# Block products of W_in and W_out in token halves of 256 columns

## What is computed

```python
# layer 0, scale and shift from a small MLP of a noise encoding of t
out = silu(scale * layer_norm(x, gamma, beta) + shift)     # mean and variance over tokens and features
out = out @ W_in + b_in                                     # 512 x 512
out = silu(scale * layer_norm(out, gamma, beta) + shift)
x2 = out @ W_out + b_out + x                                # 512 x 512
# layer 1, one expert per batch, picked by an index
h = gelu(x2 @ Wi[expert] + bi[expert])                      # 512 x 2048
r = h @ Wo[expert] + bo[expert] + x2                        # 2048 x 512
y = row_layer_norm(r) * gamma[expert] + beta[expert]
```

## Time and profile before

| | us |
|---|---|
| median of 3 runs | 1772.29 (1772.17 to 1772.65) |
| span of the profiled execution | 1771.7 |
| TensorE matmul busy | 1762.8 (99%), 7939 records |
| TensorE weight load busy | 1454.3 (82%), 7939 records |
| VectorE busy | 1286.2 (73%) |
| ScalarE busy | 977.2 (55%) |
| GpSimd busy | 69.0 (4%) |

### The profile page before, as it was taken

How to read it: one execution, slowest core, us unless ns; L and a number is a source line. 1 busy time by engine, 2 the same in 40 slices (tenths; PEclk the granted TensorE clock), 3 DMA queues, 4 the chain that set the end, 5 groups by cost and what they waited for, 6 DMA issues and landing times.

```text
span 1771.7 us, 22300 instructions
## 1 busy us (share of the span) xinstructions
PE 1762.8 (99%) x7939; PEld 1454.3 (82%) x7939; DVE 1286.2 (73%) x2147; ACT 977.2 (55%) x1551; POOL 69.0 (4%) x138
## 2 busy tenths in 40 slices
PE   9999999999999999999999999999999999999998
PEld 6888888888888888888888888888888888888887
DVE  6876777767677777767777677677777777777576
ACT  4756554565545656456564555645556555565442
POOL 1100000000000000000000000000000000000000
PEclk9999999999999999999999999999999999999999
DMA  7332232322333233232332313333133232422321
GB/s 292 99 111 75 99 111 85 143 76 99 110 120 111 75 123 110 99 110 72 122 110 99 113 69 122 112 121 110 53 139 113 98 110 75 143 87 75 114 104 68
DMA packets 51666, 189.35 MB, mean 107 GB/s; under 512 B 10467, under 2 KB 14563, under 8 KB 35044
## 3 DMA queue, kind: packets, MB, share of 16 engines
q1 hardware_dynamic: 42770, 183.94, 29.3%
q10 hardware_dynamic: 8786, 3.99, 1.8%
HBM read 171.10 MB, written 16.81 MB: 106 GB/s over the span
## 4 chain that ended last, share of the span: by engine, by line
PE 99%; DMA 1%; SPq 0%; DVE 0%; issue 0%; ACT 0%; POOL 0%; DVEq 0%
PE out_acc L553 39%; PE hid_ps L553 39%; PE blk_ps L553 18%; DMA stage<-in_cond_w 1%; SPq L365 0%; PE out_acc L583 0%; PE out_acc L594 0%; PE out_acc L595 0%; PE out_acc L598 0%; PE hid_ps L571 0%; PE blk_ps L571 0%; PE out_acc L571 0%; PE hid_ps L598 0%; PE hid_ps L594 0%; PE blk_ps L594 0%; PE hid_ps L595 0%
## 5 line engine op out<-in xcount | busy, mean ns | idle before, releaser
L553 PE MATMUL hid_ps<-x_hi,wi_lo 128*128 128x512 f32 x1020 | 396.8, 389 | 0.0
L553 PE MATMUL hid_ps<-x_lo,wi_hi 128*128 128x512 f32 x1020 | 396.8, 389 | 0.0
L553 PE MATMUL hid_ps<-x_hi,wi_hi 128*128 128x512 f32 x1020 | 396.8, 389 | 0.0
L553 PE MATMUL out_acc<-wo_hi,g_hi 128*128 128x512 f32 x1012 | 393.7, 389 | 0.0
L553 PE MATMUL out_acc<-wo_lo,g_hi 128*128 128x512 f32 x1012 | 393.7, 389 | 0.0
L553 PE MATMUL out_acc<-wo_hi,g_lo 128*128 128x512 f32 x1012 | 393.7, 389 | 0.0
L765 ACT ACTIVATE g_sb<-hid_ps,bi_sb 128x512 f32<-128x512 f32 x256 | 175.9, 687 | 311.3 <-PE hid_ps L553 311.0
L893 DVE TENSOR_TENSOR g_lo<-g_sb,g_hi 128x512 fp32r<-128x512 f32 x253 | 173.1, 684 | 190.9 <-ACT g_hi L769 189.2
L723 ACT ACTIVATE wo_hi<-stage 128x512 fp32r<-128x512 f32 x253 | 160.1, 633 | 172.1 <-PE out_acc L553 172.1
L553 PEld LDWEIGHTS hid_ps<-x_hi,wi_lo 128*128 128x128 f32 x1020 | 191.6, 188 | 39.8
L553 PEld LDWEIGHTS hid_ps<-x_hi,wi_hi 128*128 128x128 f32 x1020 | 191.6, 188 | 39.7
(11 more groups left out here) (172 smaller groups left out, 1647.9 us busy)
## 6 DMA issues: line engine op xcount, KB each, us to landing
stage<-in_expert_w SPq DMA_DIRECT2D x128, 1024.0 KB, 4.8
x<-in_xT SPq DMA_DIRECT2D x15, 1024.0 KB, 7.4
out_y<-r_sb SPq DMA_DIRECT2D x15, 1024.0 KB, 5.1
rows<-in_expert_rows SPq DMA_DIRECT2D x16, 512.0 KB, 6.7
mv_all<-mv_dram ACTq DMA_DIRECT2D x30, 128.0 KB, 3.8
affine_sb<-in_affine SPq DMA_DIRECT2D x3, 512.0 KB, 10.0
stage<-in_cond_w SPq DMA_DIRECT2D x3, 512.0 KB, 10.9
x<-in_xT SPq DMA_DIRECT2D x4, 256.0 KB, 4.5
```

Source lines behind the costliest of these rows:

```text
L553: last = pe.matmul(dst, w[wp], xs[xp], start=start and i == 0, stop=stop and i == 2)
```

## The change

`block_products` now does a whole tile: 4 chunks x 3 matmuls x 2 halves of 256 columns, 24 matmuls in one accumulation group over one bank. For W_in both halves follow each other on the same weights (order: chunk, pass, half). For W_out all 12 products of half 0 come first, then all 12 of half 1 (order: half, chunk, pass). The wait for `s_hlo` stands before the first matmul of each chunk in half 0, for m = 0. The waits for the bank and the one count of `s_blk` per tile stay.

```diff
-            def block_products(b, which, m, c):
-
-                cols = slice(m * P, (m + 1) * P)
-                return three(block_bank(b, which, m)[:, :],
-                             (w_hi[which][:, c, cols], w_lo[which][:, c, cols]),
-                             (h_hi[:, c, :], h_lo[:, c, :]), start=(c == 0), stop=(c == DC - 1))
+            def block_products(b, which, m):
+
+                bank = block_bank(b, which, m)
+                out_cols = slice(m * P, (m + 1) * P)
+                w = w_hi[which], w_lo[which]
+                h = h_hi, h_lo
+                passes = ((0, 0), (0, 1), (1, 0))
+
+                def half_product(c, n, i):
+                    wp, hp = passes[i]
+                    if m == 0 and n == 0 and i == 0:
+                        pe.wait_ge(s_hlo, splits_of(b, which, c))
+                    return pe.matmul(bank[:, HALVES[n]], w[wp][:, c, out_cols], h[hp][:, c, HALVES[n]],
+                                     start=(c, n, i) == (0, 0, 0),
+                                     stop=(c, n, i) == (DC - 1, len(HALVES) - 1, len(passes) - 1))
+
+                if which:
+                    for n in range(len(HALVES)):
+                        for c in range(DC):
+                            for i in range(len(passes)):
+                                last = half_product(c, n, i)
+                else:
+                    for c in range(DC):
+                        for i in range(len(passes)):
+                            for n in range(len(HALVES)):
+                                last = half_product(c, n, i)
+                return last
...
-                for c in range(DC):
-                    if m == 0:
-                        pe.wait_ge(s_hlo, splits_of(b, which, c))
-                    last = block_products(b, which, m, c)
-                last.then_inc(s_blk, 1)
+                block_products(b, which, m).then_inc(s_blk, 1)
```

## The result

The changed kernel takes 1798.18 us (median of 4 runs, 1798.15 to 1798.53) against 1772.23 (4 runs), a ratio of 1.0147 with a 95% interval of 1.0134 to 1.0159: 25.95 us slower. The forecast was 1796.3.

What follows compares the result with a forecast made beforehand. TensorE, busy 99% of the span, was taken as the bound. Halves +19.3 us and the h_lo wait +4.7 us sum to +24.0 on a median of 1772.29, giving 1796.3 us, range 1777 to 1810 (chance 0.84).

Steps and rivals of the forecast that it cites:

- What bounds the kernel: Whole kernel: TensorE is busy 99% of the span, so every nanosecond a product gains or loses arrives at the end.
- The halves, +19.3 us: Block products of W_in and W_out: 1440 split products, each half 120 ns, so two take 240 instead of 226.6 ns.
- Why I took 120: Half products: 106.7 ns of columns plus 13.3 per instruction, likelier a collision with the load than slow columns; chance 0.47.
- The wait for h_lo, +4.7 us: W_out's tile 0: chunk 3 is wanted before VectorE delivers it, losing 0.31 us in each of 15 batches.
- The signature: TensorE's waits list was to show h_lo of VectorE: 15 waits, near 0.3 us, all in W_out's tile 0.
- At nothing: the rest: ScalarE's and VectorE's evacuations, DMA, other queues and PSUM writes: no added time from any of them.
- 512-column products elsewhere change their 226.6 ns: Sign against the prediction: uncut products outside the block tiles no longer start 226.6 ns apart.
- Per column: Rival on half products: the extra time scales with columns, 113.3 or 114.6 ns a half, 1777.9 or 1781.4 us; chance 0.25.
- The load as the bound: Rival on half products: the weight load sets the distance, 124 ns and up, 1807 us, or 1838 at 135 ns; chance 0.19.
- The whole latency: Rival on half products: the load's whole recorded 188 ns appears between starts, +215 us, near 1987 us; chance 0.04.
- the dropped load: Rival in W_in: the repeated weight load is dropped, pairs cost 120 + 109 ns, 1788 us; chance 0.02.
- a faster half: Rival on half products: a half costs less than half a whole, 1762 us at 107.5 ns; chance 0.03.

## Why the prediction was right, by its steps

- **What bounds the kernel.** Right: TensorE without a hole, and the cost of every part of the change arrived at the end in full (26.1 accounted for, 25.95 measured).
- **The halves, +19.3 us.** Measured 18.3. The step taken was "13.3 ns per matmul, 120 ns a half", and the run with 320 and 384 columns shows that it was the right form, a cost per matmul and not per column (146.7 and 173.3 ns once steady). The missing 1.0 us is nearly all the first half of each tile or pair of tiles, 113 ns in place of 120 (116 x 7 ns = 0.8 us). If those 7 ns show one record late, as read above, they are in the term behind the tile, and the halves cost 19.1.
- **Why I took 120.** The reason given, a collision between the load and the stream, isn't shown: halves follow the load from 128 to 64 columns and not to 32, and whole products go the other way. The number stood on the comparison with plain fp32 and on one measured width. So the right number rests on a reason that these runs do not bear out, which is in part luck; what makes it 13.3 stays open.
- **The wait for h_lo, +4.7 us.** Measured 4.5 (and 4.5 back with W_out in turn). Each link was in rows of the kernel before: VectorE's end 1.22 us behind the tile's start, 0.17 from release to stream. The signature was half wrong: I looked for waits near 0.3 us in TensorE's list, and there it is 0.2 on the load side and nothing for the matmuls.
- **At nothing: the rest.** Here the term of 3.2 us was missed, 28 ns behind each of 116 tiles: the prediction took every 512-column product outside the tiles at 226.6 ns, without a row on how they run just behind other products. A sign of it was in the trace of the kernel before: in the first ticks the products of `up` start at 50.19, 50.42, 50.65, 50.88, 51.12, 51.34 and 51.58 us in its timeline, 1.39 / 6 = 232 ns apart and not 226.7. The prediction named "512-column products elsewhere change their 226.6 ns" as a sign against it, and five behind each tile did. The two errors, 1.2 too much and 3.2 too little, make the 2.0 us between 24.0 and 25.95; that they partly cancel is luck.
- **Rivals.** Per column is refuted (146.7 and 173.3 ns for 320 and 384 columns, where it wanted 141.7 and 170.0). The load as the bound asked for 124 ns or more, and a half takes 120. A load that binds takes 112, and the 13.3 ns stand at 320 and 384 columns too, where a load cannot bind, so nothing calls for it; the margin is only 8 ns, and parts of 192 are bound by it. The whole latency, the dropped load and a faster half did not occur: with full loads a tile of halves averages 119.7 ns or more for each. The Trainium skill's rule for the gap (TensorE: Matmul & The Clock Gate, Back-to-back issue gap), columns / 2.4 + 2.5 ns, which that section gives for the isolated gap, does not hold for these fp32r products at any of the four widths.

## What to carry to other kernels

Where TensorE has no idle time, cutting products in two costs its per-matmul time over the columns for each cut; take that from the distance of starts of the same data type, 13.3 ns here for fp32r with full weights against 2 for plain fp32, and not from the recorded duration. Leave room for the products behind the cut ones: here they added 28 ns for each change back, and up to 0.11 us behind quarters, some of which is the last quarter's own cost, shown late. Before reordering products so that half of the columns come first, divide the time at which each chunk is wanted by two and set it beside the times at which the other engine delivers: here 0.8 us of cover became a wait of 0.3. And check a forecast that came true against its rivals: the 64-column load alone would have led to a wrong cause.

## What the runs showed of the hardware

All at a granted clock of 1.00, on one core.

- A stream of 128-column loads runs at 111.7 ns from start to start beside fp32r and beside fp32 quarters alike; with 96 columns it is 85.0. The Trainium skill (TensorE: Matmul & The Clock Gate, LDWEIGHTS) gives columns / 1.2, 107 and 80 ns: the slope agrees, with 5 ns on top.
- A steady fp32r matmul under a full load costs 13.3 ns over its columns at 2.4 GHz, at 256, 320, 384 and 512 columns. With shorter loads it is 6.9 to 18.3 ns as a mean over a tile, depending on the pair of widths of load and stream and not steadily on either. Whole products were fastest with the full load (226.7 ns) and slower with less (230 to 232). No run here tells why.
- 512-column products at the same granted clock stand 226.7 ns apart when steady and 228 to 236 in the first five behind a tile of halves. Other shapes before them give longer or shorter transitions, up to 2.83 us for twelve products in place of 2.72. What sets it is open.
- A wait can show on the load engine alone, and with less than it costs: 2.8 us listed, 4.5 lost.
